# Another order of the pipelined steps: the next batch's key moments ahead of the second residual's projections

## The reference

```python
qn, kn = q / |q|, k / |k|                      # per head
scores = (qn @ kn.T) / temp                    # temp = sigmoid(mean(x) @ Wt + bt) + 0.5
keep the 64 largest of each row's 256 scores, softmax over them, zero elsewhere
out = (attn @ v) @ Wo + bo
x1 = layernorm(x + gate * out + (1 - gate) * x)          # gate = sigmoid(x @ Wg + bg)
x2 = layernorm(x1 + softmax((x1 Wq + bq)(c Wk + bk).T) @ (c Wv + bv))
x3 = layernorm(x2 + sum_k weights[k] * (W[ids[k]] @ x2 + b[ids[k]]))
```

## Time and profile before

| what | value |
|---|---|
| three runs, us | 3206.73, 3202.55, 3202.72 (median 3202.72) |
| profiled execution, us | 3211.29, its span 3209.3 |
| mean granted TensorE clock | 0.959 |
| busy share of the span | PE 88%, DVE 85%, ACT 66%, POOL 49% |

### The profile page before, as it was taken

One profiled execution on the slowest core, in us unless ns is written; L12 is line 12 of the kernel. 1 busy time (PEld: TensorE's weight loads), 2 busy tenths in 40 slices (PEclk: granted clock), 3 DMA queues, 4 the chain that ended last, 5 costly groups with the idle time before them and its releaser, 6 DMA issues. The chain is left out here.

```text
span 3209.3 us, 58791 instructions
## 1 busy us (share of the span) xinstructions
PE 2837.4 (88%) x16154; PEld 1560.3 (49%) x16154; DVE 2729.7 (85%) x10113; ACT 2119.9 (66%) x5970; POOL 1583.2 (49%) x2285
## 2 busy tenths in 40 slices
PE   6799999989899789998998999999988998989755
PEld 4455555545455345554554555555545554545333
DVE  4889889888888898888888898988988898888881
ACT  3577777766576557766766777777767776657541
POOL 3345555545455444554544554555545454545422
PEclk8899999999999989999999999999999999999877
DMA  6000000000000000000000000000000000000000
GB/s 226 8 18 25 25 24 22 19 10 24 24 25 22 5 24 25 25 22 4 25 25 24 25 21 25 17 13 25 25 24 22 24 18 11 24 24 18 9 10 13
DMA packets 43674, 80.04 MB, mean 25 GB/s; under 512 B 3914, under 2 KB 12106, under 8 KB 43186
## 3 DMA queue, kind: packets, MB, share of 16 engines
q1 hardware_dynamic: 41682, 69.18, 6.6%
q0 software_dynamic: 1504, 5.77, 0.5%
HBM read 58.16 MB, written 16.78 MB: 23 GB/s over the span
## 5 line engine op out<-in xcount | busy, mean ns | idle before, releaser
L523 POOL TENSOR_SCALAR probs<-probs,kept_inv 128x256 f32<-128x256 f32 x1024 | 474.0, 486 | 611.0 <-DVE kept_inv L1905 611.0
L789 ACT ACTIVATE scores<-score_ps,neg_guess 128x256 f32<-128x256 f32 x1024 | 397.5, 480 | 233.4 <-DVE kept_inv L1905 197.8
L1867 DVE SCALAR_TENSOR_TENSOR probs<-scores,threshold,probs 128x256 f32<-128x256 f32 x1011 | 434.0, 492 | 137.5 <-ACT unsure_n L815 107.5
L809 ACT ACTIVATE near<-scores 128x256 f32<-128x256 f32 x1024 | 411.3, 415 | 4.2 <-DVE nearest L1834 1.1
L824 ACT ACTIVATE probsT<-work_ps 128x512 f32<-128x512 f32 x512 | 292.7, 597 | 181.0 <-PE work_ps L1122 178.4
L1830 DVE MATCH_REPLACE8 near<-nearest,near 128x256 f32<-128x256 f32 x1024 | 406.8, 407 | 0.0
L1122 PE MATMUL work_ps<-ident,probs 128*128 128x128 f32 x2072 | 324.0, 291 | 79.2 <-POOL probs L523 36.7
L1826 DVE MAX8 nearest<-near 128x8 f32<-128x256 f32 x1024 | 358.1, 410 | 9.8 <-DVE near L1818 8.7
L1834 DVE MAX8 nearest<-near 128x8 f32<-128x256 f32 x1024 | 356.9, 409 | 0.0
L490 POOL TENSOR_TENSOR inv_norm<-sumsq,minus_half 128x32 f32<-128x32 f32 x64 | 351.2, 5488 | 5.3
L1818 DVE TENSOR_SCALAR near<-scores,flip 128x256 int32<-128x256 int32 x1024 | 307.1, 367 | 4.5
(11 more groups left out here) (173 smaller groups left out, 5484.0 us busy)
## 6 DMA issues: line engine op xcount, KB each, us to landing
x_in<-in_x_dram SPq DMA_DIRECT2D x32, 512.0 KB, 3.7
x_res<-in_x_dram SPq DMA_DIRECT2D x32, 512.0 KB, 3.6
out_dram<-rows SPq DMA_DIRECT2D x32, 512.0 KB, 3.0
c_sb<-in_ctx_dram SPq DMA_DIRECT2D x32, 256.0 KB, 2.7
rows<-in_L_ffn_W_dram SPq DMA_DIRECT2D x8, 512.0 KB, 4.7
gate_t<-in_L_ffn_W_dram SPq DMA_DIRECT2D x3, 512.0 KB, 3.7
v_sb<-in_L_ffn_W_dram SPq DMA_DIRECT2D x3, 512.0 KB, 4.5
w_q<-in_L_attn_Wq_dram POOLq DMA_DIRECT2D x1, 1024.0 KB, 8.9
```

The source lines that it names most:

```text
L523: pool.tensor_scalar(probs[:, s % 2, h, j], probs[:, s % 2, h, j], kept_inv[:, s % 2, n:n + 1], 1.0, ALU.mult, ALU.mult).then_inc(s_pr, 1)
L789: last = act.activation(scores[:, s % 2, h, j], score_ps[:, j, h], ACT.Identity, bias=neg_guess[:, t, n:n + 1])
L809: last = act.activation(near[:, h, j], scores[:, s % 2, h, j], ACT.Sign, accum_out=sign_sum[:, s % 2, n:n + 1])
L1867: step.mark(dve.scalar_tensor_tensor(out=probs[:, r, h, j], in0=scores[:, r, h, j], scalar=threshold[:, r, k:k + 1], in1=probs[:, r, h, j] ...
```

## The change

The same steps stand in another order in the written-out programs of TensorE, ScalarE and GpSimd, and in VectorE's body. The second residual's steps of batch `i - 1` (`turn_x2`, `ffn`) now stand behind the moments and products of batch `i + 1`. The body's edge has moved as well: set 2's last `turn_probs` and all of set 3's stand at the head of the next body of TensorE, and VectorE's first four steps of set 1 and set 0's `keep_top` at the end of the body before. The banks and the waits for them are redrawn to suit. Line numbers behind the tables are 2 to 6 lower than before in the changed kernel (L1841 is L1836 there, L1286 is L1280).

```diff
--- before.py
+++ after.py
@@ -330,33 +330,33 @@
-        FILL_BANK = (None, 2, 3, 0, 1, 2, 3, 0, 2, 3, 2, 0, 3, 1, 0, 3, 2)
...
+        FILL_BANK = (None, 1, 2, 0, 3, 1, 2, 0, 1, 2, 1, 0, 2, 3, 2, 1, 0)
...
@@ -568,26 +568,36 @@
                 here = where in ("first", "second", "steady", "last")
                 behind = where in ("second", "steady", "last", "drain")
                 step.restart()
-                if here:
+                if behind:
+                    out_minus_x(i - 1, 1, 1 - p)
+                    norm1(i - 1, 1 - p)
+                if here:
+                    scale_probs(i, 0, 0)
                     scale_probs(i, 0, 1)
                 if ahead:
                     if where != "fill":
                         norms(i + 1, 0)
+                if here:
+                    scale_probs(i, 1, 0)
+                if ahead:
+                    if where != "fill":
+                        norms(i + 1, 1)
                     if where != "fill":
                         normalise(i + 1, 0)
                 if behind:
                     add_x1(i - 1, 0, 1 - p)
+                if ahead:
+                    if where != "fill":
+                        normalise(i + 1, 1)
+                if behind:
                     add_x1(i - 1, 1, 1 - p)
                     norm2(i - 1, 1 - p)
                 if here:
-                    scale_probs(i, 1, 0)
-                if ahead:
-                    if where != "fill":
-                        norms(i + 1, 1)
-                    if where != "fill":
-                        normalise(i + 1, 1)
-                if here:
                     scale_probs(i, 1, 1)
+                if ahead:
+                    if where != "fill":
...
@@ -892,173 +894,165 @@
...
                     take_a(i - 1)
                 if here:
-                    copy_scores(i, 2, 0)
+                    take_unsure(i, 1)
...
@@ -1363,287 +1357,288 @@
...
+                if behind:
+                    if where == "drain":
+                        pe.wait_ge(s_x1t, at(i - 1, 2, 1))
+                    else:
+                        pe.wait_ge(s_pt, at(i, 16, 2))
+                    cross_left(i - 1)
                 if here:
                     pe.wait_ge(s_pt, at(i, 16, 1))
...
                     count_unsure(i, 1)
                     if where == "first":
                         pe.wait_ge(s_pt, at(i, 16, 2))
                     else:
+                        pe.wait_ge(s_a, at(i - 1, 1, 1))
+                    turn_probs(i, 0, 1, 0)
+                if behind:
+                    if where == "drain":
+                        pe.wait_ge(s_ct, at(i - 1, 1, 1))
+                    else:
+                        pe.wait_ge(s_fl, at(i, 4, 2))
+                    cross_scores(i - 1)
+                if ahead:
+                    if where != "fill":
+                        pe.wait_ge(s_kc, at(i + 1, 2, 2))
+                        query(i + 1, 1)
+                if here:
+                    if where == "first":
+                        pe.wait_ge(s_fl, at(i, 4, 2))
+                    else:
+                        pe.wait_ge(s_s2, at(i - 1, 1, 1))
+                    turn_probs(i, 0, 1, 1)
+                if behind:
+                    pe.wait_ge(s_x1t, at(i - 1, 2, 2))
+                    turn_cross(i - 1)
...
@@ -1952,62 +1947,60 @@
                 here = where in ("first", "second", "steady", "last")
                 behind = where in ("second", "steady", "last", "drain")
                 step.restart()
+                if here:
+                    turn_to_guess(i, 1, 1)
                 if ahead:
                     if where != "fill":
                         query_sums(i + 1, 0)
                 if here:
-                    choose_sides(i, 1)
-                    turn_to_guess(i, 1, 0)
-                    keep_top(i, 0)
+                    search(i, 1, 1)
+                if ahead:
+                    if where != "fill":
+                        temperature(i + 1)
+                if here:
+                    set_threshold(i, 1)
                 if ahead:
                     if where != "fill":
                         key_sums(i + 1, 0)
                 if here:
-                    search(i, 1, 0)
-                if ahead:
-                    if where != "fill":
-                        temperature(i + 1)
+                    keep_top(i, 1)
                 if behind:
                     cross_max(i - 1)
-                if here:
-                    turn_to_guess(i, 1, 1)
+                if ahead:
+                    if where != "fill":
+                        key_sums(i + 1, 1)
+                if here:
+                    choose_sides(i, 2)
                 if behind:
                     cross_scale(i - 1)
-                if here:
-                    search(i, 1, 1)
                 if ahead:
                     if where != "fill":
                         query_sums(i + 1, 1)
                 if here:
-                    set_threshold(i, 1)
-                    choose_sides(i, 2)
                     turn_to_guess(i, 2, 0)
+                    turn_to_guess(i, 2, 1)
                     search(i, 2, 0)
-                    keep_top(i, 1)
-                if behind:
-                    cross_statistics(i - 1, 1 - p)
-                if here:
-                    turn_to_guess(i, 2, 1)
                     search(i, 2, 1)
-                if ahead:
-                    if where != "fill":
-                        key_sums(i + 1, 1)
-                if here:
                     set_threshold(i, 2)
                     choose_sides(i, 3)
                     turn_to_guess(i, 3, 0)
-                    turn_to_guess(i, 3, 1)
+                if behind:
+                    cross_statistics(i - 1, 1 - p)
+                if here:
                     search(i, 3, 0)
                     keep_top(i, 2)
+                if ahead:
+                    if where != "fill":
+                        query_moments(i + 1, 0)
+                    if where != "fill":
+                        query_moments(i + 1, 1)
+                if here:
+                    turn_to_guess(i, 3, 1)
+                if ahead:
+                    if where != "fill":
+                        moments(i + 1)
+                if here:
                     search(i, 3, 1)
-                if ahead:
-                    if where != "fill":
-                        query_moments(i + 1, 0)
-                    if where != "fill":
-                        query_moments(i + 1, 1)
-                    if where != "fill":
-                        moments(i + 1)
-                if here:
                     set_threshold(i, 3)
                     keep_top(i, 3)
                 if behind:
@@ -2021,6 +2014,11 @@
                     set_threshold(i + 1, 0)
                 if here:
                     mixing(i, p)
+                if ahead:
+                    choose_sides(i + 1, 1)
+                    turn_to_guess(i + 1, 1, 0)
+                    keep_top(i + 1, 0)
+                    search(i + 1, 1, 0)
 
             setup()
             split_biases(0)
```

More of the change, by code:

```diff
@@ L1398, in body @@
                     if where != "fill":
-                        pe.wait_ge(s_xt, at(i + 1, 2, 2))
-                        temp(i + 1)
+                        if where == "first":
+                            pe.wait_ge(s_v, at(i, 2, 1))
+                        else:
+                            pe.wait_ge(s_pt, at(i - 1, 16, 16))
+                        turn_x(i + 1, 1)
+                    if where != "fill":
+                        pe.wait_ge(s_xt, at(i + 1, 2, 1))
+                        query(i + 1, 0)
                     if where != "fill":
@@ new lines, in body @@
+                if here:
+                    pe.wait_ge(s_pt, at(i, 16, 8))
+                    count_unsure(i, 3)
+                    if where == "first":
+                        pe.wait_ge(s_kt, at(i + 1, 2, 2))
+                    else:
+                        pe.wait_ge(s_f, at(i - 1, 2, 1))
+                    attend(i, 1, p)
+                    if where == "first":
+                        pe.wait_ge(s_pt, at(i, 16, 7))
+                    else:
+                        pe.wait_ge(s_f, at(i - 1, 2, 2))
+                    turn_probs(i, 2, 0, 0)
+                    pe.wait_ge(s_fl, at(i, 4, 4))
+                    turn_probs(i, 2, 0, 1)
+                    pe.wait_ge(s_at, at(i, 4, 2))
@@ L2010, in body @@
                 if here:
+                    search(i, 3, 1)
                     set_threshold(i, 3)
```

641 lines of the change are left out of this document (293 added, 348 removed).

## The result

The changed kernel takes 3213.24 us (median of 8, 3211.82 to 3220.86) against 3205.68 us before (8 runs, 3202.55 to 3207.63): ratio 1.0029, 95% interval 1.0018 to 1.0040. It is slower, as forecast, but by 8 us and not by 37.

The account below looks back on a forecast made before the run. TensorE was taken to bound the body, only just, with VectorE nearly full: 84.9 + 4.1 + 1.1 + 2.4 = 92.5, less 0.5, is 92.0 us a body, +37 us over 31 bodies, 3240 us; range 3165 to 3300.

Parts of the forecast that it names:

- terms 1 and 2: TensorE's list without waits, 84.9 us a body, plus 4.1 of waits from the new order: 89.0, 1.8 less than now.
- the 0.5: Us a body taken off the 92.5 sum, since the same walk gave VectorE's earlier body 91.5 against 90.5 measured.
- term 4: GpSimd's normalise and add_x1 hold up VectorE's set_threshold of set 2, add_x2 that of set 3: +2.4 us a body.
- term 3: VectorE's loop edge, now between set 1's halves, makes turn_cross late in half the bodies: +1.1 us on the mean.
- the head: TensorE's waits at the body's start, round set 2's last turn, attend and set 3's turns: 0.8 and 1.0 us.
- the moments' hand-offs: TensorE's five hand-offs at the moments' steps and turn_x2 add 0.6 us a body.
- A: GpSimd's large steps miss VectorE's set_threshold: 90.1 us a body, 3181 us and faster; chance 0.22.
- C: Loop edge and GpSimd's hold on VectorE eat the gain: 90.6 to 91.0 us a body, about 3203; chance 0.11.

Follow-up runs that it names:

- both GpSimd edits: Changed kernel, VectorE's loop written out; GpSimd runs both normalise together, scale_probs of set 1 before add_x1, of set 2 before add_x2: 3159.3 us, ratio 0.9847.
- the cross edit: Changed kernel, loop written out; TensorE's turn_probs, attend and scores reordered round the cross-attention's softmax to fill two waits: 3229.1 us, ratio 1.0068.
- all five edits: Written-out changed kernel with both GpSimd reorders, set 2's count later, set 3's first turn before attend, and the cross edit: 3163.6 us, ratio 0.9867.

## Why the prediction was right in sign and wrong in size

In us a body. The first measured column spreads the whole time over the 31 bodies (difference of ratios x 3206 / 31; each is good to some 0.2). The second compares clean bodies: 88.7 us with neither meeting, 90.1 with both (90.0 over the six bodies of the table), 90.9 with the loop as well, 90.8 before.

| step | forecast | whole run | clean bodies |
|---|---|---|---|
| terms 1 and 2 less the 0.5, against 90.8 | -2.3 | -1.6 (both GpSimd edits, no loop) | -2.1 |
| term 4 | +2.4 | +0.6 (0.9847 to 0.9902) | +1.4 |
| term 3 | +1.1 | +1.3 (0.9902 to 1.0029) | +0.9 |
| sum | +1.2 | +0.3 | +0.1 |

The whole-run figure of term 4 is too low and that of terms 1 and 2 too small a gain, since the edits behind them took the meeting away in ten clean bodies only. Term 4 was measured without the loop; with the loop in place nobody took the meeting away.

**Term 4 is the step that failed.** The mechanism was right, instruction by instruction, and so was the price of a wait of TensorE: 1.46 us of it are worth 1.4. The wait was put at 2.4 us. For set 2 the forecast had 1.9 us and the trace has 1.05. On VectorE the stretch was 2.0 us, where the walk had 2.3 to 2.8 (its own two parts, 1.2 and 1.0 to 1.25, add up to no more than 2.2 to 2.45). And VectorE was 1.0 us and not 0.7 ahead of TensorE, so that only the rest reached the count. For set 3 it was 0.4 and not 0.5. This 1.0 us a body too much is, in clean bodies, nearly the whole error of the forecast.

**Terms 1 and 2** came out at 88.7 us, where the forecast had 89.0 - 0.5 = 88.5, but not part by part. TensorE's waits in two of the ten clean bodies without the meeting:

```profile
PE work_ps L1292 <- ACT probsT L822: 2.7, 5, 0.8
PE work_ps L1112 <- ACT rows L849: 1.7, 2, 0.9
PE work_ps L1112 <- DVE rows L1931: 1.5, 2, 1.1
```

That is 3.0 us a body and not 4.1: `take_a` came with 0.9 as walked, the head with 1.3 to 1.4 (forecast 1.8), `turn_cross` with 0.4 to 1.1 for 0.8, the moments' hand-offs with nothing for 0.6. What is left, 85.7 us, was put at 84.9 (by its own numbers 90.6 - 4.9 - 1.0 = 84.7). The two errors and the 0.5 that was taken off, for a walk of VectorE's steps whose working is not given, cancel; that is luck.

What terms 1 and 2 leave out is VectorE's own list. Its waits in a body without the loop:

```profile
DVE probs L1862 <- ACT unsure_n L817: 3.6, 2, 2.0
DVE sq L1782 <- PE work_ps L1255: 0.5, 1, 0.5
DVE kept_inv L1900 <- DVE probs L1862: 0.4, 1, 0.4
```

The first row is the round trips behind the counts of sets 1 (2.0) and 3 (1.6). From `keep_top` of set 1 to set 3's count VectorE runs without a gap but for the 0.5 us ahead of `query_moments`. Filling 1.7 us of TensorE's waits in that stretch brought much of it back as a longer wait for set 2's count; with the clock and ScalarE's `take_query` in the way, no run shows what the filling alone is worth.

**Term 3** has nearly the right sum for partly another reason. I took the old edge's 3.0 us; in the new place three queued maxima hide 1.1 of them. The lateness also ends as a wait for set 1's count (1.75 us in body 4) and not at `turn_cross`, where the forecast looked for some 3 us. The rest came through the clock, which the forecast did not have: a late count of 1.6 to 2.6 us is paid once as a wait, and at seven of thirteen edges again as 3.4 us at half speed. That the old edge cost nothing is shown (0.9996 without it).

**The sign** was right by little. The forecast had 1.2 us a body, clean bodies show 0.1, and the 8 us of the whole run are under 0.3% of it; it could as well have come out the other way.

**Rivals.** A ("the large steps miss `set_threshold`") did not happen. C, terms 3 and 4 eating the gain, is nearest: it had 90.6 to 91.0 us a body, and 90.9 were measured. The order by itself does win, 90.0 us a body with the meeting and 88.7 without; VectorE's loop takes 0.9 back.

What stays open: why VectorE's return from the branch takes 2.8 us in one place and 3.5 in another; why bodies with a doubtful head gain 0.5 to 3 us from the written-out loop, which the gaps alone don't give, and hardly anything from the other edits; and what VectorE's 1.3 us of longer `keep_top` cost.

## What to carry to other kernels

Where two engines are both nearly full, ask of each wait why it is there. A wait that went because its cause went was won in full in the bodies where it went (1.46 us of wait, 1.4 us of time). A wait that was filled with other work ahead of a point where the second engine is late came back at that point.

An edit that moves a long instruction off one step moves it onto another: look in several bodies where it lands, since only ten of twenty were rid of the meeting here. And price a gain by the bodies that have it, not by all of them.

A wait that is made longer can cost twice when TensorE's clock falls behind it. A hardware loop's edge belongs where its engine waits anyway; if the program has room, write the loop out.

## What the hardware showed that was not expected

- In the kernel with the cross edit 23 of 25 TensorE waits of 1.7 to 2.0 us, outside bodies with a doubtful head, were followed by 3.4 us at half clock. The same length of wait did not always do it: behind thirteen edges with waits of 1.6 to 2.6 us it was seven, and with all five edits three of ten waits of 1.5 to 1.7 us. What decides is not shown. Without the loop and without further edits none of the 20 clean bodies has such a stretch.
- VectorE works off its queue beyond its loop's branch (up to 2.2 us of work); the sequencer is back 2.7 to 3.7 us after the branch.
- Beside GpSimd, a VectorE instruction that reads two tiles is held to the end of the one GpSimd instruction: 1.2 us beside one of 1.9, 0.1 us beside ones of 0.5. An instruction of 128x8 was held as one of 128x128 was (1.24 us in place of 0.16). The power on 32 columns is the exception: 5.46 us, and nothing held.
